# Single-row TensorE products in turned column groups, one fold product per tile

## The reference

```
mean  = sum_t m[t] * x[t,:] / (sum_t m[t] + 1e-6)          (masked mean)
q     = mean @ Wq.T ;  k = x @ Wk.T ;  v = x @ Wv.T
score = (q . k[t]) / sqrt(128) + log(exp(-alpha*a[t])*m[t] + 1e-12), -inf where not m
long  = softmax(score) @ v
short = mean of the last 5 masked-in rows of x
g     = sigmoid(mean popularity and age of those 5 rows @ gate_w.T + gate_b)
y     = layernorm(g*short + (1-g)*long) * gamma + beta
```

## Time and profile before

| What | Value |
|---|---|
| Runs | 206.36, 208.58, 211.24 us (median 208.58) |
| Profiled execution | 206.09 us, span 204.4 us |
| VectorE busy | 174.1 us, 85% of the span |
| TensorE matmul busy / weight load busy | 168.8 us, 83% / 102.9 us, 50% |
| GpSimd busy | 143.0 us, 70% |
| ScalarE busy | 118.8 us, 58% |
| Mean granted TensorE clock | 0.946 of full speed |
| DMA | 55.19 MB, mean 270 GB/s |

### The profile page before, as it was taken

The page is one execution under the profiler, slowest core; times in us unless marked ns, Lnnn a source line. Parts: engine busy times, 40 slices in busy tenths (PEclk is TensorE's granted clock), DMA queues, the critical chain, the costliest instruction groups (busy, mean ns, idle before and its releaser), DMA issues.

```text
span 204.4 us, 6882 instructions
## 1 busy us (share of the span) xinstructions
PE 168.8 (83%) x2005; PEld 102.9 (50%) x2005; DVE 174.1 (85%) x1332; ACT 118.8 (58%) x646; POOL 143.0 (70%) x167
## 2 busy tenths in 40 slices
PE   0172864887999699899999999999999999997890
PEld 0132432444565456565655565656565656564570
DVE  0513989989999999999899999898999998989703
ACT  2002255587767377667676777676677776768410
POOL 3467982488959587777869887769698877486311
PEclk9998555699999999999999999999999999999998
DMA  7949969996888878988988899988888998600000
GB/s 36 303 153 304 257 223 420 418 431 287 311 293 326 325 268 287 339 328 277 333 311 331 345 330 338 321 318 323 311 328 287 386 363 313 246 2 14 0 3 13
DMA packets 15683, 55.19 MB, mean 270 GB/s; under 512 B 10160, under 2 KB 11312, under 8 KB 11568
## 3 DMA queue, kind: packets, MB, share of 16 engines
q1 hardware_dynamic: 15088, 53.64, 74.2%
q0 software_dynamic: 576, 1.33, 2.2%
HBM read 54.70 MB, written 0.26 MB: 269 GB/s over the span
## 4 chain that ended last, share of the span: by engine, by line
POOL 31%; issue 25%; PE 17%; DVE 14%; DMA 8%; ACT 3%; POOLq 1%; ACTq 0%; SPq 0%; DVEq 0%
POOL gprod L286 14%; DVE junk_v L686 9%; PE ps_sum L358 6%; POOL mblk L266 6%; DMA x<-in_r_hist_items_dram 5%; POOL pblk L275 5%; PE ps_wx L358 4%; DMA mask_p<-in_r_hist_mask_dram 3%; PE ps_sum L368 3%; PE ps_query L377 2%; POOL pop_taken L344 2%; POOL age_taken L344 2%; ACT sums L467 1%; POOL taken L322 1%; PE ps_group L386 1%
## 5 line engine op out<-in xcount | busy, mean ns | idle before, releaser
L686 DVE SCALAR_TENSOR_TENSOR junk_v<-x,ps_query 128x128 f32<-128x128 f32 x576 | 127.2, 277 | 7.5 <-ACT query L485 7.3
L286 POOL TENSOR_TENSOR gprod<-x,query 128x512 f32<-128x512 f32 x64 | 71.9, 1144 | 32.0 <-ACT query L485 31.9
L458 ACT ACTIVATE gprod<-gprod 128x128 f32<-128x128 f32 x224 | 66.1, 299 | 2.7 <-DVE kept L653 1.4
L358 PE MATMUL ps_wx<-x,pblk 128*32 128x256 f32 (+1 forms) x832 | 67.2, 380 | 0.0
L358 PE MATMUL ps_sum<-x,mblk 128*32 128x256 f32 (+1 forms) x832 | 63.5, 404 | 3.2 <-DMA x<-in_r_hist_items_dram 3.1
L358 PEld LDWEIGHTS ps_sum<-x,mblk 128*32 128x32 f32 (+1 forms) x832 | 34.2, 115 | 25.0 <-issue 7.0
L686 DVE DVE_READ_ACCUMULATOR junk_v<-x,ps_query 128x1 f32 x576 | 45.9, 80 | 0.0
L458 ACT ACTIVATION_READ_ACCUMULATOR gprod<-gprod 128x1 f32 x224 | 42.7, 190 | 0.0
L467 ACT ACTIVATE sums<-ps_sum,rcnt_rows 128x256 f32<-128x256 f32 x32 | 15.1, 472 | 29.9 <-PE ps_sum L358 29.9
L275 POOL TENSOR_TENSOR pblk<-own,ex 128x400 f32<-128x400 f32 x32 | 27.4, 875 | 6.1 <-ACT ex L493 6.1
L358 PEld LDWEIGHTS ps_wx<-x,pblk 128*32 128x32 f32 (+1 forms) x832 | 25.0, 107 | 12.6
(11 more groups left out here) (94 smaller groups left out, 100.4 us busy)
## 6 DMA issues: line engine op xcount, KB each, us to landing
x<-in_r_hist_items_dram SPq DMA_DIRECT2D x32, 1600.0 KB, 8.8
age_p<-in_r_hist_age_hours_dram SPq DMA_DIRECT2D x1, 400.0 KB, 14.6
out_dram<-y SPq DMA_DIRECT2D x4, 64.0 KB, 4.2
mask_p<-in_r_hist_mask_dram SPq DMA_DIRECT2D x1, 100.0 KB, 6.1
mask_u<-in_r_hist_mask_dram SPq DMA_DIRECT2D x1, 100.0 KB, 3.5
wq<-in_L_rec_Wq_dram SPq DMA_DIRECT2D x1, 64.0 KB, 5.7
wk<-in_L_rec_Wk_dram SPq DMA_DIRECT2D x1, 64.0 KB, 3.8
wv<-in_L_rec_Wv_dram SPq DMA_DIRECT2D x1, 64.0 KB, 3.7
```

Of the source, the lines that this page charges most:

```text
L286: nc.gpsimd.tensor_tensor(gprod[:, t, a * D:b * D].rearrange("p (r d) -> p r d", d=D), rows((k % GP) * PAIR + t, r0 + a, r0 + b), query[:, ...
L358: ins = nc.tensor.matmul(dst[c:c + n * TU, 0:n * D], blk[:, k % 2, t, 2 * m:2 * m + n, :].rearrange("p r u -> p (r u)"), x[:, i + t, 2 * m ...
L458: ins = nc.scalar.activation(src, src, ACT.Copy, accum_out=score[:, k % 2, t, DOTS + r:DOTS + r + 1])
L686: ins = V.scalar_tensor_tensor(out=junk_v[:, t, r, :], in0=x[:, (k % GP) * PAIR + t, r * D:(r + 1) * D], scalar=1.0, in1=c_query[t], op0=A ...
```

## The change

`sum_rows` takes one row per product: 16 weight columns and 128 columns of x, 25 products for a tile. The result of a column group has 16 rows of 128 columns, all wanted. `sums`, `wx` and `fold` are half as wide, ScalarE's two copies read 128 columns, and `make_mean` and `fold_rows` need one product per tile where they had two. The column group of product m is (m + col) % 4, where col is 0 or 1 by kind of sum and t (SUM_COL, WX_COL). The cuts of the weighted sums are at rows 7 and 15 (t = 0) and 3 and 11 (t = 1) of 25. At t = 1, `fold_rows` stands behind the first part of the weighted sums, next to `make_mean`. The upper 16 partitions of each column group of 32 are no longer written, so VectorE clears the four PSUM banks once at the start (DVE_BANKS), and TensorE waits for that before its first step.

```
-NPROD = (ROWS + 1) // 2
-CUT_SUMS, CUT_MEAN = 4, 8
+CUTS = ((7, 15), (3, 11))
+SUM_COL, WX_COL = (0, 0), (1, 1)
...
-        fold = sb("fold", [P, 2, TU])
+        fold = sb("fold", [P, TU])
-        sums = sb("sums", [P, PAIR, 2 * D])
+        sums = sb("sums", [P, PAIR, D])
-        wx = sb("wx", [P, PAIR, 2 * D])
+        wx = sb("wx", [P, PAIR, D])
...
-            def sum_rows(dst, blk, i, k, t, ms=range(NPROD)):
-                for m in ms:
-                    n = min(2, ROWS - 2 * m)
-                    c = 32 * (m % CG)
-                    ins = nc.tensor.matmul(dst[c:c + n * TU, 0:n * D],
-                                           blk[:, k % 2, t, 2 * m:2 * m + n, :].rearrange("p r u -> p (r u)"),
-                                           x[:, i + t, 2 * m * D:(2 * m + n) * D],
-                                           start=(m < CG), stop=(m >= NPROD - CG))
+            def sum_rows(dst, blk, i, k, t, col, a=0, b=ROWS):
+                for m in range(a, b):
+                    c = 32 * ((m + col) % CG)
+                    ins = nc.tensor.matmul(dst[c:c + TU, 0:D], blk[:, k % 2, t, m, :], x[:, i + t, m * D:(m + 1) * D],
+                                           start=(m < CG), stop=(m >= ROWS - CG))
...
             def make_mean(s, t):
-                for rr in range(2):
-                    ins = nc.tensor.matmul(c_mean[t], sums[:, t, rr * D:(rr + 1) * D], fold[:, rr, :],
-                                           start=(rr == 0), stop=(rr == 1))
-                ins.then_inc(mean_done, 1)
+                nc.tensor.matmul(c_mean[t], sums[:, t, :], fold[:, :], start=True, stop=True).then_inc(mean_done, 1)
...   (fold_rows: in the same way one product for each t)
             def step(g, k):
                 for t in range(PAIR):
                     back, u = (3, 1) if t == 0 else (2, 0)
+                    cut_sums, cut_mean = CUTS[t]
                     if has(s, 0):
                         masked_sums(s, g, k, t)
+                    if has(s, back):
+                        weighted_sums(s - back, k - back, u, 0, cut_sums)
                     if t == 1 and has(s, 3):
                         fold_rows(s - 3, PUSERS * ((k - 3) % GP), wx).then_inc(wx_folded, 1)
-                    if has(s, back):
-                        weighted_sums(s - back, k - back, u, range(CUT_SUMS))
                     if has(s, 0):
                         make_mean(s, t)
...
+            pe.wait_ge(dve_setup, DVE_BANKS)
             steps(pe, step, NPAIR + 3)
...   (ScalarE: copies of ps_sum and ps_wx read 0:D where they read 0:2 * D)
+            for unused in ps_sum + ps_wx:
+                link(V.memset(unused[:, 0:D], 0.0))
```

More of the change, by code:

```diff
@@ L63 @@
 POOL_CONSTANTS = 15
+DVE_BANKS = 4
 def build(nc, items, mask, age, pop, Wq, Wk, Wv, gate_w, gate_b, gamma, beta, decay_alpha, out):
@@ L308, in _ @@
             build_mblk(0, 0)
-            link(nc.gpsimd.memset(fold[:, :, :].rearrange("p a u -> p (a u)"), 0.0))
+            link(nc.gpsimd.memset(fold[:, :], 0.0))
             for c in range(CG):
-                select(fold[:, :, :], ALU.not_equal, [[-TU, 2], [-1, TU]], -32 * c, 1, 1.0)
+                select(fold[:, :], ALU.not_equal, [[-1, TU]], -32 * c, 1, 1.0)
             link(nc.gpsimd.memset(ones[:, :], 1.0))
@@ L384, in fold_rows @@
                     pe.wait_ge(wx_copied, s * PAIR + t + 1)
-                    for rr in range(2):
-                        ins = nc.tensor.matmul(ps_group[:, c + t * TU:c + (t + 1) * TU], src[:, t, rr * D:(rr + 1) * D],
-                                               fold[:, rr, :], start=(rr == 0), stop=(rr == 1))
+                    ins = nc.tensor.matmul(ps_group[:, c + t * TU:c + (t + 1) * TU], src[:, t, :], fold[:, :],
+                                           start=True, stop=True)
                 return ins
@@ L394, in masked_sums, with weighted_sums @@
                     pe.wait_ge(sum_copied, (s - 1) * PAIR + t + 1)
-                sum_rows(ps_sum[t], mblk, k * PAIR, k, t).then_inc(sum_done, 1)
-            def weighted_sums(s, k, t, ms=range(NPROD)):
-                if ms[0] == 0:
+                sum_rows(ps_sum[t], mblk, k * PAIR, k, t, SUM_COL[t]).then_inc(sum_done, 1)
+            def weighted_sums(s, k, t, a, b):
+                if a == 0:
                     pe.wait_ge(pblk_ready, s * PAIR + t + 1)
@@ L401, in weighted_sums @@
                         pe.wait_ge(wx_copied, (s - 1) * PAIR + t + 1)
-                ins = sum_rows(ps_wx[t], pblk, (k % GP) * PAIR, k, t, ms)
-                if ms[-1] == NPROD - 1:
+                ins = sum_rows(ps_wx[t], pblk, (k % GP) * PAIR, k, t, WX_COL[t], a, b)
+                if b == ROWS:
                     ins.then_inc(wx_done, 1)
@@ L421, in step @@
                     if has(s, back):
-                        weighted_sums(s - back, k - back, u, range(CUT_SUMS, CUT_MEAN))
+                        weighted_sums(s - back, k - back, u, cut_sums, cut_mean)
                     if has(s, 0):
@@ L425, in step @@
                     if has(s, back):
-                        weighted_sums(s - back, k - back, u, range(CUT_MEAN, NPROD))
+                        weighted_sums(s - back, k - back, u, cut_mean, ROWS)
                     if t == 0 and k == 2 and has(g, 1, NGROUP):
@@ L466, in copy_sums @@
                     act.wait_ge(mean_done, (s - 1) * PAIR + t + 1)
-                nc.scalar.activation(sums[:, t, :], ps_sum[t][:, 0:2 * D], ACT.Copy,
+                nc.scalar.activation(sums[:, t, :], ps_sum[t][:, 0:D], ACT.Copy,
                                      scale=rcnt_rows[:, bass.ds(s * PAIR + t, 1)]).then_inc(sum_copied, 1)
@@ L473, in copy_weighted @@
                 act.wait_ge(wx_done, s * PAIR + t + 1)
-                nc.scalar.activation(wx[:, t, :], ps_wx[t][:, 0:2 * D], ACT.Copy).then_inc(wx_copied, 1)
+                nc.scalar.activation(wx[:, t, :], ps_wx[t][:, 0:D], ACT.Copy).then_inc(wx_copied, 1)
             def copy_mean(s, t):
@@ L777, in step @@
                         dots(s, k, 0, i, i + 1)
+            for unused in ps_sum + ps_wx:
+                link(V.memset(unused[:, 0:D], 0.0))
+            assert made[0] == DVE_BANKS
             link(V.memset(pmax[:, :], 0.0))
```

## The result

Four runs of the changed kernel gave 217.36 to 220.56 us, median 220.19; four of the kernel before, 206.36 to 211.24, median 207.62. The ratio is 1.060, 95% interval 1.046 to 1.073: the change makes this kernel 6% slower. The forecast was 203.8 us, its range ended at 210. Executions of one kernel can lie some per cent apart: the ratios and intervals here leave out those more than 1.5% above the kernel's fastest, the medians do not. The profiled execution took 220.56 us, its span is 218.8, against 206.09 and 204.4 before.

A forecast was written before the change was run, and what follows sets the result against it. TensorE was taken as the bound by little, VectorE right behind. Start 0.4, even stretch 3.3 and tail 1.0 us sum to 4.7, from 206.09 to 201.4 us profiled, 203.8 us as median; 8-in-10 range 199.5 to 210.

The forecast's parts named there:

- Code is fetched again in the loop: Rival: TensorE's longer loop body no longer stays, so it stalls twice at the loop's turn; 205 to 207 us, chance 0.08.
- The price of a stop: At TensorE's loop turn: 1.2 us per code block, one or two blocks awaited at each of two turns, 2.4 to 5 us.
- What the kernel can absorb: At the loop's turn: VectorE's long half step at the first pair of a group covers part of TensorE's 2.4 to 5 us.
- Narrow passes keep pace: TensorE's single-row products: 27 ns a pass assumed, TensorE the bound again above 34; the slower rival had chance 0.13.
- The sum of the gain: Whole kernel: start 0.4, even stretch 3.3 and tail 1.0 us, together 4.7 us less.
- the copy `sums`: ScalarE's copy before the mean at t = 0: shrinks from 0.47 us toward 0.27, near 0.30, saving 0.17 us per pair.
- the even stretch: VectorE's waits for the query from 45.7 to 180 us, 3.6 + 0.3 us, of which 3.3 were expected to go.
- VectorE is the next bound: In the loop after the change: one loop pass near 39.6 us, with TensorE waiting for VectorE's `dots_done`.
- The rival of its own stretch: VectorE's operations sharing time with GpSimd stretch; 2 to 3 of 3.3 us return, 206 us; chance 0.17 together with late loads.
- The tail: The end, where VectorE is done and TensorE sets the time: shorter folds and an earlier ScalarE copy save 1.0 us.
- The start: Before the even stretch: one early VectorE wait, on the chain sums, copy, mean, query, shrinks by 0.4 us.

The follow-up runs named there:

- e5: The changed kernel with eight one-column products (32 instructions) ahead of TensorE's loop, body untouched: 0.989 of the kernel before, 207.2 us.
- e6: The kernel before, wide products, TensorE's loop body padded to 1,713 instructions and 50 tiny products (200 instructions) ahead of the loop: 1.139 of before, 238.1 us.
- e11: The changed kernel with three tiny products (12 instructions) ahead of TensorE's loop: median 225.4 us, before 207.8, no interval.
- e1: The changed kernel with TensorE's looped steps written out, other engines keeping their loops: 0.973 of the kernel before, median 204.1 us.
- e12: The changed kernel with TensorE's looped steps written out, run again on another chip: 0.987 of the kernel before, median 205.3 us.
- e9: The changed kernel, TensorE written out, VectorE with 17 dot products per tile instead of 18 and 24 single-column clears at its start: 0.984 of before, 204.5 us.
- e8: The changed kernel, TensorE written out, VectorE with 17 dot products per tile instead of 18, GpSimd with ScalarE 8 instead of 7: 1.022 of before, 214.0 us.
- e2: The kernel before, wide products, with TensorE's looped steps written out: 1.003 of the kernel before.

## Why the prediction was wrong

**The step that failed** is the rival "Code is fetched again in the loop": its chance, 0.08, and its price, 2.4 to 5 us. I named the place (TensorE's stall at the loop's turn) and the sign by which it would be seen (blocks on the instruction queue between 110 and 190 us), and both came true: 15 blocks. It went wrong in three places.
- *It was ruled out by length.* I compared 1,704 and some 40 register instructions with a room of 2,048, "with less than two blocks to spare". The body has 1,744, as I counted. But what is held is blocks, and a loop of 6.8 blocks' length touches 7 or 8, by where it begins. It was 8, and 8 don't stay: e5, e6 and e11 show it in either direction. The margin of less than two blocks was the warning: where the beginning is unknown, a body of L instructions can touch one block more than L/256 rounded up. And the trace of before showed no more than that 5 blocks stay.
- *The price of a stop.* I took 1.2 us per block, from the queue's share of 16 engines, and one or two blocks per turn. Measured: 5.58 + 3.24 us at the first turn, 8.8 us, and 5.94 + 2.55 at the second, 8.5 us. The share says how long packets kept engines busy, not how long an engine waits for them. And it is not one or two blocks: e5, the same code with a loop that stays, moved 13 blocks, the changed kernel 31. That is 9 more for each of two turns, the loop's eight and one, so by the count the whole loop was fetched again. TensorE stood still at two places only, the branch and the first boundary; the blocks behind them went on arriving while it worked (four between 121 and 150 us).
- *What the kernel can absorb.* I had VectorE's long step at the first pair of a group cover part of it. It did so, a little: of 8.8 us VectorE lost 8.0, of 8.5 us 7.8.

The Trainium skill, "Runtime: NRT & Kernel Launch", section on instruction fetch mechanics, says that a taken branch whose target is outside the window of two blocks has to wait until the target is fetched; the trace agrees that such a wait exists, 6.0 and 6.4 us. It also says that TensorE has room for 2,048 instructions, and that "The IRAM is only 2 cache lines". The runs agree with neither as a rule for a loop: one that touches 7 blocks turned in 0.22 us (and already the 5 blocks of the kernel before are more than two), and one that touches 8, which are 2,048, did not stay.

**Narrow passes keep pace: right.** 49 in 1.59 us in e1, 32 ns each, with weight loads between them. Without the last pass's own 0.27 us it is 27.5 ns from one to the next, where I had put 27 and the limit at 34. The Trainium skill ("TensorE: Matmul & The Clock Gate", section on what happens when you issue a matmul) gives 62 ns for each MATMUL without hardware decode, which would make 3.0 us of these 49, an estimate; the trace doesn't agree.

**The sum of the gain: about right in e1, when the loop's turn is taken out; not settled.** Forecast 4.7 us on the profiled execution's scale, 0.4 + 3.3 + 1.0. e1 against before: first `kept` 38.1 for 38.3 (0.2), the 15 pairs 147.0 for 151.4 (4.4), tail 199.1 - 185.1 = 14.0 for 14.7 (0.7): 5.3 us. Within it, the copy `sums` shrank from 472 ns to 367, not to near 300; so its 0.17 us of the sum was at most 0.11. That e1 comes so near to the sum is in part luck, since it is the fastest of four executions, 200.86 to 209.4 us. The profile of e12, the same kernel, gives 204.4 - 203.9 = 0.5 us: first `kept` 2.2 us later, the 15 pairs 150.9 (0.5 less), the tail 12.5 (2.2 less). In ratios, 0.973 and 0.987 for one kernel, where the forecast was 0.977; the 3.3 us of the even stretch are not shown by both.

**VectorE is the next bound: right for e1, not so cleanly elsewhere.** In e1 its waits for the query between 45.7 and 180 us are gone, and TensorE waits for `dots` instead (5.1 us in six waits), as forecast. The rival of its own stretch is real too. In e5 its busy time is 180.8 us against e1's 174.6, and one instruction shows most of it (groups over the span: busy us, mean ns; e1 first, then e5, and then e5's timeline):

```profile
L650 DVE TENSOR_TENSOR kept<-score,hide 128x50 f32<-128x50 f32 x16 | 9.5, 595 | 0.1
```

```profile
L653 DVE TENSOR_TENSOR kept<-score,hide 128x50 f32<-128x50 f32 x16 | 14.4, 901 | 0.1
```

```profile
115.14 4.00 DVE L653 TENSOR_TENSOR kept<-score,hide 128x50 f32<-128x50 f32 x1
...
121.56 0.46 PE L372 MATMUL ps_query<-wqk,mean_p 128*128 128x128 f32 x2 [3.60 <-DVE junk_v L686]
```

The same instruction that takes 0.2 us at best took 4.00 once, and behind it TensorE waited 3.60 us for `dots`. In the kernel before its mean is 425 ns. e5's 15 pairs took 155.8 us where e1's took 147.0, with loops that turn in 0.22 us; `kept` has 4.9 of these 8.8 us, the rest is not assigned. What `kept` waits for inside its own duration isn't shown: GpSimd had two products in flight for 2.24 us of it, from 115.19 us, but that they hold it up is only a guess.

**The tail: no gain in the changed kernel** (14.7 and 14.7), 0.7 to 2.4 in e1, e12 (203.9 - 191.4 = 12.5) and e5 (206.2 - 193.9 = 12.3), forecast 1.0.

**The start** has a piece that no step named. ScalarE's first copy of `sums` started at 16.8 us in the kernel before and at 16.7 in e1, but at 22.0 in the changed kernel and in e12. The two lines are the changed kernel's and e1's:

```profile
21.96 0.37 ACT L463 ACTIVATE sums<-ps_sum,rcnt_rows 128x128 f32<-128x128 f32 x1 [4.80 <-remote]
```

```profile
16.67 0.35 ACT L464 ACTIVATE sums<-ps_sum,rcnt_rows 128x128 f32<-128x128 f32 x1
```

Since e1 and e12 are one kernel, the change doesn't bring it about by itself. It goes with the chip: the four profiles from e12's chip (e9 to e12) have it at 21.4 to 22.0 us, the eight from the two chips of e1 to e8 at 16.2 to 18.1. By the first `kept` most of it is regained (39.8 us in the changed kernel and 40.5 in e12, for 38.3). What ScalarE waits for is put down to "remote", that is to nothing in the trace, and stays open; it may be part of the distance between 0.973 and 0.987.

## What to carry to other kernels

Before lengthening the body of a hardware loop, count its instructions on each engine from the built program and ask how many blocks it touches at the worst beginning: here 7 of 256 instructions stayed on TensorE and 8 didn't, and, with the beginning assumed, 3 of 128 stayed on VectorE and 4 didn't. On TensorE the loss was 7.6 to 10.5 us a turn. The sign is in two lines, the duration of TensorE's taken branch (0.2 us, or 4.0 to 6.4) and the blocks on the instruction queue inside the loop. On VectorE only the second shows, with waits for issue: in e8 its branches stayed at 72 ns at most. If the body is near the edge, write the steps out or move the loop by a few instructions ahead of it, and measure a change to the loop in both forms, since the sign of the result can be the boundary's and not the change's.

## What the hardware showed that I had not expected

- A stop at a loop's turn comes in two parts: at the branch (5.58 us on TensorE), and again at the first block boundary behind it (3.24 us); in e6, 3.17 and 4.51. Where that boundary is 5 instructions away, in e11, they are one stop of 9.25 us.
- Straight code seems not to be free of stops when it runs through quickly. Written out, with nearly twice the instructions per tile of the kernel before, TensorE has short gaps that are put down to "issue": in e1 2.4 us in four before `ps_wx`, in e12 4.8 us in four before `ps_sum`. From 60 to 195 us e2, written out with wide products, shows none, and e5, whose loop stays, has 0.2. That they are late blocks is argued from this and the name alone.
- After a stop TensorE runs at a lower clock for a while. In the changed kernel 0.89 was granted from 102.8 to 150.8 us, where 1.00 had been granted in a loop pass of before; in this time TensorE had stood for 5.58 and 3.24 us. From 110 to 120 us it was 0.71, and 40 passes behind the second stop took 2.34 us where e1's 49 took 1.59. From 120 to 150 us it was 1.00 again. A stop is not needed for it, though: from 50 to 60 us 0.83 was granted with TensorE busy for 9.75 of 10 us.
